# Expert masks of the first batch spread by TensorE into PSUM instead of through DRAM, early maxima filled one unit ahead, and new places for the side work

## The reference, cut to what matters

```python
# block 0: attention with one head of 32 dimensions, causal
h = layernorm(x) * (1 + ca) + sa
x = x + ga * softmax(causal(q k^T / sqrt(32))) @ (h @ (Wvdown @ Wvup))
# block 0: experts; one of 8 experts for each token
h = layernorm(x) * (1 + cb) + sb
probs = softmax(h @ Wg + bg);  idx = argmax(probs);  p = probs[idx]
x = x + gb * p * relu(h @ We[idx % 8] + be[idx % 8])
# block 1: attention, 16 heads of 8 dimensions, over all 1024 tokens
h = layernorm(x) * (1 + ca) + sa
x = x + ga * (softmax(q k^T) v @ Wout^T + bout)
# block 1: two linear layers without a nonlinearity between them
h = layernorm(x) * (1 + cb) + sb
x = x + gb * ((h @ W1[b]^T + b1[b]) @ W2[b]^T + b2[b])
```

## Time and profile before

| | us |
|---|---|
| three runs, median | 1722.59 (1719.32 to 1724.51) |
| the profiled execution | 1724.31 |
| its span, first to last instruction | 1722.7 |
| TensorE busy in the span | 1631.0 |
| VectorE busy | 1484.0 |
| ScalarE busy | 1327.3 |
| GpSimd busy | 820.2 |

### The profile page before, as it was taken

How to read it: one execution, slowest core, us unless ns; L and a number is a source line. 1 busy time by engine, 2 the same in 40 slices (tenths; PEclk the granted TensorE clock), 3 DMA queues, 4 the chain that set the end, 5 groups by cost and what they waited for, 6 DMA issues and landing times.

```text
span 1722.7 us, 61469 instructions
## 1 busy us (share of the span) xinstructions
PE 1631.0 (95%) x26588; PEld 735.5 (43%) x26588; DVE 1484.0 (86%) x2254; ACT 1327.3 (77%) x1798; POOL 820.2 (48%) x1157
## 2 busy tenths in 40 slices
PE   6999999999999999989999999999999999999998
PEld 3765443434434443434334343434434343333335
DVE  5649988899889998999989998989989998989973
ACT  4432678887888878877898888878888878877885
POOL 2444346834675366834676265744677263101110
PEclk9999999999999999999999999999999999999999
DMA  2111211012210321012210222012210222001101
GB/s 74 52 44 48 63 53 42 24 40 76 78 42 16 99 65 56 19 44 76 79 37 19 75 69 73 20 47 77 61 39 24 62 63 76 25 24 51 47 16 35
DMA packets 83306, 87.52 MB, mean 51 GB/s; under 512 B 9452, under 2 KB 67484, under 8 KB 83036
## 3 DMA queue, kind: packets, MB, share of 16 engines
q1 hardware_dynamic: 82492, 83.07, 16.3%
q10 hardware_dynamic: 544, 0.52, 0.1%
HBM read 61.02 MB, written 21.99 MB: 48 GB/s over the span
## 4 chain that ended last, share of the span: by engine, by line
PE 69%; ACT 13%; POOL 7%; DVE 6%; issue 3%; SPq 1%; DMA 0%; ACTq 0%; POOLq 0%
PE pv_psum L819 24%; PE side_psum L541 15%; PE buffer L804 12%; ACT p L1052 9%; PE buffer L794 7%; DVE row_max L1374 3%; PE pv_psum L829 2%; POOL rest L1490 2%; PE buffer L541 2%; POOL s L1498 1%; PE side_psum L598 1%; PE side_psum L631 1%; POOL x L1548 1%; ACT o_sb L1061 1%; ACT hT_f L932 1%
## 5 line engine op out<-in xcount | busy, mean ns | idle before, releaser
L1374 DVE TENSOR_REDUCE row_max<-buffer 128x2 f32<-128x1024 f32 x1024 | 1223.1, 1218 | 115.0 <-PE buffer L794 103.8
L1052 ACT ACTIVATE p<-buffer 128x1024 f32<-128x1024 f32 x1024 | 1038.6, 1024 | 196.2 <-PE buffer L804 184.8
L819 PE MATMUL pv_psum<-p,v 128*9 128x256 f32 x8192 | 578.2, 384 | 3.2 <-ACT o_sb L1061 2.6
L794 PE MATMUL buffer<-k_ops,q_ops 24*128 24x512 f16 x2048 | 398.6, 386 | 42.9 <-ACT p L1052 38.8
L804 PE MATMUL buffer<-q_ops,k_ops 26*128 26x512 f16 x2048 | 397.6, 386 | 9.4 <-DVE row_max L1374 8.0
L819 PEld LDWEIGHTS pv_psum<-p,v 128*9 128x9 f32 x8192 | 156.0, 89 | 236.4 <-issue 153.9
L804 PEld LDWEIGHTS buffer<-q_ops,k_ops 26*128 26x128 f16 x2048 | 95.8, 91 | 347.6 <-issue 212.1
L1498 POOL TENSOR_SCALAR s<-s,nm 128x1024 f32<-128x1024 f32 (+6 forms) x56 | 145.3, 2595 | 55.5 <-DVE nm L1220 55.5
L1515 POOL TENSOR_TENSOR hm<-masks,hT_f 128x1024 f32<-128x1024 bf16 x56 | 119.7, 2148 | 95.5 <-PE side_psum L541 77.4
L794 PEld LDWEIGHTS buffer<-k_ops,q_ops 24*128 24x128 f16 x2048 | 96.0, 91 | 151.8 <-ACT p L1052 127.6
L541 PE MATMUL side_psum<-we,hm 128*32 128x128 f32 x3648 | 121.2, 274 | 0.0
(11 more groups left out here) (319 smaller groups left out, 1746.1 us busy)
## 6 DMA issues: line engine op xcount, KB each, us to landing
masks<-masks_rows SPq DMA_DIRECT2D x16, 1024.0 KB, 5.6
q_ops<-products SPq DMA_DIRECT2D x256, 48.0 KB
k_ops<-products SPq DMA_DIRECT2D x256, 48.0 KB
attention<-o_sb SPq DMA_DIRECT2D x248, 18.0 KB
x<-in_L_attn_inputs SPq DMA_DIRECT2D x8, 512.0 KB, 4.5
products<-q_parts SPq DMA_DIRECT2D x16, 256.0 KB, 2.3
w_sb<-in_L_ffn_W SPq DMA_DIRECT2D x16, 256.0 KB, 3.4
out<-x SPq DMA_DIRECT2D x16, 256.0 KB, 2.4
```

Of the source, the lines that this page charges most:

```text
L794: m = e.matmul(buffer[:, hh, :], q_ops[rows, slot, of, i * P:(i + 1) * P], k_ops[rows, slot, of, halves(half)[1]], start=True, stop=True)
L819: m = e.matmul(pv_psum[q:q + VW, half * QUARTER:(half + 1) * QUARTER], v1[b % 2][:, kb, 2 * hp + hh, :], p_sb[n % KEPT][:, hh, part * QUAR ...
L1052: e.activation(p_sb[n % KEPT][:, :, :], unit("exp", n)[0][:, :, :], ACT.Exp, scale=over_scale[n // (2 * PERIOD)]).then_inc(S["exp_done"], 1)
L1374: e.tensor_reduce(mx[pair % 2][:, :, i, half], unit("max", n)[0][:, :, :], axis=AX.X, op=ALU.max).then_inc(S["max_done"], 1)
```

## The change

1. For batch 0 the stages `hm`, `masks_out` and `masks_load` are gone. In their place are 16 stages `mask 0 t part`. On TensorE each multiplies a column of the identity, repeated over 128 columns, by the tile's columns of `onehotT`, for four experts, which puts the expert's row on all partitions of a PSUM bank. On VectorE each multiplies that bank by `hT_f`. The products of batch 0 go into `hm_first`, four tiles of 128 x 8 x 128 in the memory of `masks`, which batch 0 does not use now; a tile waits for `moe` of tile t - 4. Later batches keep their way through DRAM.
2. `maxima_at`: before step 0 TensorE fills one maxima unit more than the step's own, so units 0 and 1 at step -32 and none at step -1. VectorE's order is the same.
3. The tables are new: `PLACES` (94 of 191 places), `ALONE`, `COUNTED`, `SWITCH` (1 to 3.4), `LIGHT` (5.4 to 7.8), `ZEROS_AHEAD` and `ZEROS_BESIDE`.

```diff
+EARLIER = 1
-SWITCH, LIGHT = 1, 5.4
+SWITCH, LIGHT = 3.4, 7.8
...
--15 maxima 0, -18 nm_split 0, -6 nm 0, -1 maxima 1, -1 nm_split 1, 4 nm 1, 20 maxima 2, 18 nm_split 2, 22 nm 2, 36 maxima 3, 36 nm_split 3, 38 nm 3,
+-16 maxima 0, -7 nm_split 0, -11 nm 0, 0 maxima 1, 1 nm_split 1, 5 nm 1, 16 maxima 2, 15 nm_split 2, 25 nm 2, 35 maxima 3, 34 nm_split 3, 38 nm 3, 48
...
+def maxima_at(h):
+    if h >= 0:
+        return range(h + 2 * LEAD, min(h + 2 * LEAD + 1, PAIRS * UNITS))
+    due = [min(h + 2 * LEAD + ahead, 2 * LEAD) for ahead in (EARLIER, EARLIER + 1)]
+    return range(0 if h == -2 * LEAD else due[0], due[1])
...
+    hm_first = masks[:, :, :].rearrange("c k n -> c (k n)").bitcast(F32).rearrange("c (s k q) -> c s k q", k=EXPERTS, q=P)
+    def hm_of(b, t):
+        return hm[t % 2] if b else hm_first[:, t % 4, :, :]
...
+        def mask_stage(b, t, part):
+            v = empty(("mask", b, t, part))
+            emptied("onehotT", b, t // 4)
+            pe.wait_ge(S["ident_bf"], 1)
+            for j in range(4):
+                k = 4 * part + j
+                m = tiled(v[:, j * P:(j + 1) * P], ident_bf[:, k:k + 1].broadcast_to([P, P]), onehotT[:, t * P:(t + 1) * P], True, True)
+            m.then_inc(S["side_filled"], 1)
...
-            if h + 2 * LEAD < PAIRS * UNITS:
-                max_scores(h + 2 * LEAD)
+            for n in maxima_at(h):
+                max_scores(n)
...
-        def hm_stage(b, t):
-            if b:
-                return
+        def mask_stage(b, t, part):
+            v = filled("mask", b, t, part)
             dve.wait_ge(S["side_act"], side["channels", b, 1, t // 4].emptied)
-            dve.wait_ge(S[f"masks_in{t // 4}"], 16)
-            if t >= 2:
-                dve.wait_ge(S["side_filled"], side["moe", b, t - 2].filled)
-            cols = slice(t * P, (t + 1) * P)
-            e.tensor_tensor(hm[t % 2][:, :, :], masks[:, :, cols], hT_f[:, cols].unsqueeze(1).broadcast_to([C, EXPERTS, P]),
-                            op=ALU.mult).then_inc(S["hm"], 1)
+            if t >= 4:
+                dve.wait_ge(S["side_filled"], side["moe", b, t - 4].filled)
+            e.tensor_tensor(hm_of(b, t)[:, 4 * part:4 * part + 4, :], v.rearrange("p (k q) -> p k q", q=P),
+                            hT_f[:, t * P:(t + 1) * P].unsqueeze(1).broadcast_to([C, 4, P]), op=ALU.mult).then_inc(S["side_dve"], 1)
```

More of the change, by code:

```diff
@@ L116 @@
[L116 to L119, removed]
@@ new lines @@
+0, -196 stats 0 0 1 1, -192 apply 0 0 0, -194 apply 0 0 1, -192 channels 0 0 0, -188 g0 0 0, -193 channels 0 0 1, -189 g0 0 1, -191 v0 0, -190 later
+0, -190 gates 0, -187 scores 0 0 0, -186 softmax 0 0, -187 exp0 0 0, -185 scores 0 1 0, -184 transpose_p 0 0 0, -184 softmax 0 1, -185 exp0 0 1, -182
+scores 0 2 0, -181 transpose_p 0 1 0, -181 softmax 0 2, -180 times_v 0 0, -182 exp0 0 2, -179 scores 0 3 0, -177 transpose_p 0 2 0, -177 softmax 0 3,
+-178 times_v 0 1, -178 exp0 0 3, -176 scores 0 4 0, -175 scores 0 4 1, -174 transpose_p 0 3 0, -172 transpose_p 0 3 1, -172 softmax 0 4, -173 times_v
@@ L187 @@
[L187 to L188 removed]
+apply 0 0 1, gates 0, channels 0 0 0, softmax 0 0, channels 0 0 1, g0 0 0, scores 0 0 0, softmax 0 1, v0 0, scores 0 1 0, stats 0 0 1 0, exp0 0 0,
+scores 0 2 0, stats 0 0 0 0, softmax 0 2, stats 0 0 1 1, exp0 0 1, later 0, scores 0 3 0, transpose_p 0 0 0, softmax 0 3, g0 0 1, exp0 0 2,
@@ new lines @@
+1, moe_a 0 1, onehotT 0 1, index 0 1 1, scores 1 0 0, gates 1, onehot 0 1, mask 0 3 1, moe 0 1, mask 0 4 0, scores 1 1 0, moe_a 0 2, moe 0 2, mask 0 4
+1, mask 0 5 0, mask 0 5 1, inverse 0, mask 0 6 0, moe_a 0 3, powers 0, moe 0 3, residual 0 0, mask 0 6 1, over_gating 0 1, stats 0 2 0 0, mask 0 7 0,
+moe_a 0 4, softmax 1 0, exp0 1 0, stats 0 2 0 1, moe 0 4, apply 0 2 0, exp0 1 1, mask 0 7 1, moe_a 0 5, moe 0 5, parts 0 0 0, channels 0 2 0, moe_a 0
+6, qk1 0 0 0, qk1 0 1 0, moe 0 6, softmax 1 1, later 1, moe_a 0 7, moe 0 7, parts 0 1 0, residual 0 1, v1 0 0, stats 0 2 1 0, stats 0 2 1 1, scores 1
@@ L199, in make_plan @@
             h, stage = at + 2 * b * PERIOD, (name, b * HEADS // 2 + n if pairs else b, *more)
-            if stage in first:
+            if stage in first or b == 0 and name in STRAIGHT_MASKS:
                 continue
@@ L927, in channels @@
                 act.wait_ge(S["side_filled"], side["v1", b - 1, half].filled)
-            if which == 2:
-                act.wait_ge(S["hm"], b * T + 4 * half + 4)
+            if which == 2 and b == 0:
+                act.wait_ge(S["side_dve"], side["mask", b, 4 * half + 3, 1].emptied)
+            elif which == 2:
+                act.wait_ge(S["hm"], (b - 1) * T + 4 * half + 4)
             block, j = divmod(which, 2)
@@ L1666, in masks_load @@
             cols = halves(half)[1]
-            sp.wait_ge(S[f"masks_out{half}"], 16 * (b + 1))
-            if b:
-                sp.wait_ge(S["hm"], (b - 1) * T + 4 * half + 4)
+            sp.wait_ge(S[f"masks_out{half}"], 16 * b)
+            if b == 1:
+                sp.wait_ge(S["side_filled"], side["moe", 0, T - 1].filled)
+            else:
+                sp.wait_ge(S["hm"], (b - 2) * T + 4 * half + 4)
             e.dma_start(masks[:, :, cols], masks_dram[:, cols].unsqueeze(0).broadcast_to([C, EXPERTS, BANK])).then_inc(S[f"masks_in{half}"], 16)
```

90 lines of the change are left out of this document (45 added, 45 removed), and 39 rows, old and new, of tables (COUNTED, ZEROS_AHEAD, ZEROS_BESIDE).

## The result

The changed kernel takes 1727.8 us in the median (1723.3 to 1735.3, 12 runs), the kernel before 1721.5 us (1717.6 to 1725.7, 12 runs) beside it: a ratio of 1.0040, 95% interval 1.0025 to 1.0056. So it is 4 to 10 us slower. The time lies inside my range by luck, for its upper end was set for rival (b); the forecast of 1721.2 us and of no measurable difference was wrong. The profiled execution has a span of 1729.6 us, 6.9 us above that of before.

The account below looks back on a forecast made before the run. Three stretches: TensorE's order or the k_ops load ends the first, VectorE limits the second, TensorE is nearly always busy in the third. Terms -1.0 - 0.3 - 0.3 + 0.2 = -1.4 us gave 1721.2 us, range 1713 to 1730.

Parts of the forecast that it names:

- rival (b): Middle batches: new places make the order rougher, nine more steps cost 8.1 us, 1729.3 us in all; chance 0.17.
- What bounds the kernel: Whole kernel: three stretches, the first ended by TensorE's order or the k_ops load within 3 us, the second by VectorE.
- Part 1: Batch 0: the removed DRAM route of the masks takes 7.0 us, twice, but is not 14 us of gain.
- Part 2: First stretch, TensorE: 16 added mask stages cost 3.9 us, from 3.2 to 8.4.
- Rival (c): First stretch: masks cost TensorE 8.4 us for 3.9, first maxima come later, 1725.7 us in all; chance 0.09.
- Part 3: First stretch, VectorE: sixteen mask products from PSUM instead of eight cost +1.2 us, hidden by idle time.
- Part 4: TensorE's order in the first stretch: first maxima come 1.0 us sooner, ends -3 to +4.5.
- Part 5: Maxima one unit ahead before step 0: -0.3 us, ends -1.1 and +1.2; more fillers add 2.4 us against 2.3 to spare.
- Parts 6 and 7: End: -0.3 us from fewer fillers, +0.2 in the last batch; middle with new places and weights: 0.
- (a): Middle batches: new places make the order smoother, seven batches give 7 us, 1714.2 us in all; chance 0.28.

Follow-up runs that it names:

- e12: e9 with batch 0's masks by store and load over DRAM again and the 15 fillers ahead of mask stages gone; 1722.2 us, ratio 1.0002.
- e5: The kernel before with only batch 0's masks spread by TensorE; 1728.3 us, ratio 1.0034.
- e9: The changed kernel with the product qk1 0 1 1 and the store of k_parts moved forward, VectorE's order untouched; 1725.8 us, ratio 1.0015.
- e2: The kernel before with qk1 0 1 1, v1 0 1 and the split and store of k_parts moved back; 1729.2 us, ratio 1.0034.
- e3: The changed kernel with the maxima no longer one unit ahead; 1729.0 us, ratio 1.0044.
- e6: The changed kernel with places, planner weights, corrections and fillers of steps 0 and later as in the kernel before; 1728.5 us, ratio 1.0035.
- e7: The changed kernel with 170 fillers instead of 191 in steps -32 to -1; 1726.3 us, ratio 1.0026.
- e8: The changed kernel with 33 more fillers ahead of the first maxima, in TensorE's wait for the load; 1729.5 us, ratio 1.0047.
- e10: e9 with 170 fillers instead of 191 in steps -32 to -1; 1724.6 us, ratio 1.0022.
- e11: e10 with the maxima no longer one unit ahead; 1724.6 us, ratio 1.0016.

## Why the prediction was wrong

**What bounds the kernel** was right: three stretches, the first ended by TensorE's order or by the load within 3 us of it, the second by VectorE. The sentence on the two ends, TensorE's order and the load, was the decisive one, and I didn't follow it up.

**Part 1** was right: the masks' DRAM route was worth little, and with it back e12 is 3.5 us shorter in A, the 15 fillers included.

**Part 2** was right in its size: 3.9 us forecast, 4.0 us more of busy time measured in both pairs (e5 against before, e9 against e12). Two stages in 0.56 us are 32 matmuls at 18 ns, 4.5 us for all 16 stages. The Trainium skill (TensorE: Matmul & The Clock Gate, Back-to-back issue gap) gives about 81 ns a pair, an estimate of 20.7 us for the masks; the runs disagree. Rival (c), the upper price, did not come.

**Part 3** was right: the products take 0.68 us each, 1.25 for two in a row, and are hidden.

**Part 4 failed**, and the load is the step that failed: the prediction named it as the second end of the first stretch, used it in part 4 only as a lower end of the range, and put its delay in the new order at nothing without a reason. What the runs showed in its place is below, after the smaller miss.

The smaller miss is TensorE's order. Its sum took away idle time as a lump, part of it on guess. By its terms the stretch from onehotT 0 0 to the first maxima held 71.7 + 3.9 - 2.4 = 73.2 us of work and, for the -1.0, 1.3 us of idle time. Stretch A up to the end of TensorE's own work, changed kernel:

```profile
58.61:134.90 76.29, 74.32 (x1524) 51.66 (x1515) 36.94 (x120) 26.88 (x66) 35.77 (x62) 1.00 0.09 29
```

76.3 us for the 75.5 of before, 74.3 of work and 2.0 idle: 1.1 and 0.7 us over my terms, +0.8 where I had -1.0. The 2.95 us of idle time in my sum began at 60 us and left out 0.89 us ahead of that; in the whole of A it was 3.8 us before. Only 0.1 of the 1.1 us of work is the masks, and I can't name the rest. In the idle time stand 0.70 us in which TensorE waited at 112.09 us for the norm that I worked out. GpSimd in the changed kernel:

```profile
104.38 1.94 POOL L1527 TENSOR_SCALAR s<-s,nm 128x384 f32<-128x384 f32 x1 [6.78 <-DVE nm L1252]
...
109.05 0.19 POOL L1431 TENSOR_SCALAR sm_f<-mv_f 128x4 f32<-128x4 f32 x1
```

sm_f slipped by 1.3 us, not by 0.3: the subtraction that I had put at 103.4 us started at 104.38 and took 1.94 us for 1.57.

The larger miss is the load. I carried only TensorE's order to the new kernel. The new order moved qk1 0 1 1 back behind four other stages of TensorE, from 114.39 to 120.29 us, and with it the split, the store behind a copy in ScalarE's queue, and the load. I never wrote down where that stage had gone, though the order shows it. Nor did I price the chain from store to arrival: in the five kernels in which TensorE waited for the load (changed, e2, e3, e6, e7) it took 3.4 to 5.2 us from the store's issue to the load's, 6.0 to 8.5 from there to the first matmul. By the least of these, 6.0 us, the load of before, issued at 126.41, arrived at 132.4 us or later: an estimate of at most 1.7 us of slack before 134.10, where the store alone came 2.9 us later. In the kernels with late operands the wait came to 1.2 to 3.9 us, and the clock behind it cost up to 1.6 us more in the changed kernel (e8) and 3.5 in e7 (B of 50.5 against e10's 47.1, which has the same fillers at full clock).

**Part 5** had the wrong sign for the early maxima by themselves in the kernel before (+1.5 to +1.9 for -0.3), the right size with the changed places (+0.1, e10 against e11). The extra fillers cost 0.8 (e9's 47.9 against e10's 47.1). TensorE has 46.6 us of work in 47.9 there: the extra 2.4 us used up the 2.3 us to spare, as that sentence feared.

**Parts 6 and 7** stood: end and middle are neutral within 0.5 us. Rivals (a) and (b) did not come. (b) gave nearly the right time, 1729.3 for 1727.8, by luck: its mechanism, a rougher middle, is not in the trace.

**The sum as the runs have it.** The changed kernel lost 7.1 us up to the recurring place: 4.8 in stretch A (order with masks +0.8, wait for the load +3.9) and 2.4 in B (clock +1.6, fillers +0.8). The order with masks is itself two terms, +3.5 of masks with their 15 fillers, and so about -2.7 of all else in the new order, where 36 other fillers are gone (4.1 us). This is the sum of one execution; the wait and the clock vary from one to the next, by up to 2.7 and 3.5 us. In ratios: the changed kernel stands at 1.0040, with the operands early 1.0015, with the masks over DRAM too 1.0002.

Five points are open. Why the same store and load take 10.6 us once and 13.3 another time is not shown. Nor is the 1.0 us of work in A that I can't name. Whether the clock falls behind a gap of 1.2 us was different in e3 and e7, and no run here separates what decides it. The total of e5 lies some 3 us above what its recurring place shows. And e9's median lies 1.3 us above its bracket, for which I have no cause beside the width of its interval.

## What to carry to other kernels

When an order changes, follow every stage that feeds the next bound, through each queue that it passes, to the instruction that waits. A chain that is "not much earlier" than the bound is a second bound: price it in full, transfers included, for they show no wait as long as they are just in time. Here a transfer that hardly anything waited for was cheaper than 4 us of work on the critical path. To bring a transfer forward, move its issue, and don't let a busy in-order engine wait for it ahead of others' work.

## What the runs showed of the hardware

The same store and load, in the same program up to there, took 10.6 us from the store's issue to the first matmul that reads them in e3 (125.49 to 136.11) and 13.3 in the changed kernel (125.53 to 138.87); 1.4 us of the difference are the store's time to its landing (3.4 and 4.8). And a short idle time of TensorE can cost more than itself: in e7 a gap of 1.2 us was followed by about 10 us at the lower clock (137.7 to 148) and 3.5 us of loss, while 33 fillers in a gap of 3.9 us kept the clock up and saved 1.6 us. Matmuls of 32 weight columns in four column tiles, 128 columns of bf16, ran at 18 ns each with their weight loads (32 in 0.56 us).
